# A graph network's first convolution: every 61st pair of edge blocks fetched row by row from ScalarE's queue

## What is computed

```python
def gcn_conv(x, src, dst, W, b, n):
    h = x @ W
    s, d = concatenate([src, arange(n)]), concatenate([dst, arange(n)])
    dinv = rsqrt(max(degree(d), 1))
    msg = h[s] * (dinv[s] * dinv[d])[:, None]
    return segment_sum(msg, d, n) + b
x1 = relu(batch_norm(gcn_conv(x, src, dst, W1, b1, n), g1, be1))   # 256 -> 128
x2 = relu(batch_norm(gcn_conv(x1, src, dst, W2, b2, n), g2, be2))  # 128 -> 64
out = relu(concatenate([x, x1, x2]) @ Wfc + bfc)
```

## Time and profile before

| | us |
|---|---|
| median of 3 runs | 8550.78 |
| lowest and highest | 8532.67, 8573.71 |
| the profiled execution's own time | 8529.07 |
| its span, first to last instruction | 8527.4 |
| busy in the span: PE, PE weight loads, DVE | 4861.2, 3596.1, 3516.2 |
| busy in the span: ACT, POOL | 2055.2, 4850.5 |
| mean granted TensorE clock | 0.691 of full speed |

### The profile page before, as it was taken

One profiled execution on the slowest core, in us unless ns is written; L12 is line 12 of the kernel. 1 busy time (PEld: TensorE's weight loads), 2 busy tenths in 40 slices (PEclk: granted clock), 3 DMA queues, 4 the chain that ended last, 5 costly groups with the idle time before them and its releaser, 6 DMA issues. The chain is left out here.

```text
span 8527.4 us, 116975 instructions
## 1 busy us (share of the span) xinstructions
PE 4861.2 (57%) x27409; PEld 3596.1 (42%) x27410; DVE 3516.2 (41%) x8745; ACT 2055.2 (24%) x5831; POOL 4850.5 (57%) x4806
## 2 busy tenths in 40 slices
PE   3677777777777777843343343333544444444444
PEld 2444555444555445542333333333434434444434
DVE  6565665556655556671222222222312222222224
ACT  4444554444444445550000000000100000000001
POOL 2644444444444444456666666666366666666665
PEclk9788888888888888985555555555655555555555
DMA  7654454445444545451111111111211111111114
GB/s 221 207 145 142 143 145 143 144 141 146 142 143 144 146 143 148 139 154 53 46 46 46 46 45 46 46 46 46 53 28 29 29 29 29 29 29 29 30 25 134
DMA packets 515807, 783.35 MB, mean 92 GB/s; under 512 B 143368, under 2 KB 392453, under 8 KB 514957
## 3 DMA queue, kind: packets, MB, share of 16 engines
q0 software_dynamic: 176176, 377.82, 17.4%
q1 hardware_dynamic: 303390, 369.82, 13.9%
q10 hardware_dynamic: 35758, 30.37, 1.1%
HBM read 695.07 MB, written 82.51 MB: 91 GB/s over the span
## 5 line engine op out<-in xcount | busy, mean ns | idle before, releaser
L1703 POOL DMA_INDIRECT c_g<-conv_table,c_idx x3128 | 3029.1, 968 | 1640.4 <-issue 897.0
L1782 PE MATMUL c_sums<-c_g,acc 128*128 x7040 | 1660.7, 399 | 2108.5 <-issue 1488.6
L1010 POOL DMA_INDIRECT acc<-gat_table,ga_idx x1564 | 1539.4, 984 | 1754.2 <-DVE ga_wg L1271 1252.3
L1782 PEld LDWEIGHTS c_sums<-c_g,acc 128*128 128x128 f32 x7040 | 1499.6, 299 | 2367.2 <-issue 2313.0
L1744 DVE TENSOR_TENSOR acc<-acc,c_sums 128x128 f32 (+1 forms) x1760 | 443.8, 252 | 3420.7 <-DMA ga_h<-h_parts 1111.7
L1396 PE MATMUL ga_sums<-ga_wg,ga_S 128*128 128x265 f32 x3520 | 1160.3, 454 | 266.1 <-issue 226.0
L1346 PE MATMUL ga_dstp<-ga_oht,ga_h 128*128 128x256 bf16 x5280 | 859.9, 303 | 338.5 <-DVE ga_prod L1192 199.7
L1396 PEld LDWEIGHTS ga_sums<-ga_wg,ga_S 128*128 128x128 f32 x3520 | 692.8, 218 | 504.8 <-issue 348.7
L1346 PEld LDWEIGHTS ga_dstp<-ga_oht,ga_h 128*128 128x128 bf16 x5280 | 558.1, 108 | 721.4 <-issue 279.5
L1050 ACT ACTIVATE acc<-ga_encp 128x512 f32<-128x512 f32 x880 | 518.8, 589 | 1338.6 <-remote 793.8
L1192 DVE SCALAR_TENSOR_TENSOR ga_prod<-acc,ga_a_dst,ga_dstp 128x512 f32<-128x512 f32 x880 | 647.6, 736 | 248.8 <-issue 167.8
(11 more groups left out here) (253 smaller groups left out, 3826.7 us busy)
## 6 DMA issues: line engine op xcount, KB each, us to landing
ga_h<-h_parts SPq DMA_DIRECT2D x880, 192.0 KB
ga_dl<-dl_rows SPq DMA_DIRECT2D x110, 512.0 KB
c_g<-conv_table,c_idx POOLq DMA_INDIRECT x3128
acc<-gat_table,ga_idx POOLq DMA_INDIRECT x1564
h_parts<-h_split SPq DMA_DIRECT2D x14, 1344.0 KB
gat_table<-h_out SPq DMA_DIRECT2D x14, 952.0 KB
x_rows<-md_x SPq DMA_DIRECT2D x14, 896.0 KB
fc_x<-x_rows ACTq DMA_DIRECT2D x98, 128.0 KB
```

Of the source, the lines that this page charges most:

```text
L1010: pool.indirect_dma_start(G[:, (v * PC + j) * HROW:(v * PC + j + 1) * HROW], None, gat_table, bass.IndirectOffsetOnAxis(idx[:, c:c + 1], 0 ...
L1703: pool.indirect_dma_start(G[:, c % (2 * SLOTS), :], None, table, bass.IndirectOffsetOnAxis(idx[:, c:c + 1], 0)).then_inc(rows_in[c // 2 % ...
L1782: last = nc.tensor.matmul(sums[:, b % R, 0:width], S[:, u * CH + 2 * b + j, :], flat[:, bass.ds(slots[b] * (2 * width) + j * width, width) ...
```

## The change

It concerns the first convolution alone; the second runs the code as before.

- Of the 782 pairs each one whose number is 60 modulo 61 (12 pairs: 60, 121, ... 731) is a "single"; the other 770 stay with POOL, which issues 1540 gathers, not 1564. G gets two more slots, 20 and 21, which the singles use in turn.
- ACT fetches a single in 256 DMAs of one row of 512 B, each from the row whose number is in a register. It first loads the 256 numbers into SBUF in two small DMAs (L1706 of the changed kernel), and takes them from there into registers, eight at a time (L1652). From the third single on it waits until PE has done the single two before, whose buffer it takes.
- SP's loop is written out. The same releases and announcements follow each other in straight code, with the free numbers loaded eight at a time. Right after the announcement of the pair ahead of a single, SP waits for all 256 rows of it (a semaphore that rises by 4096 each time) and announces it.
- The unit table gets a fifth row, the slot number with the singles taken out of the ring; 21 more small DVE operations in `units_phase` work it out, chained one after another. PE reads that row in c1.
- The free list of c1 leaves the singles out of the blocks and has them at its end; it comes in three DMAs, and the three rows of the table in three.

The diff, cut:

```diff
+SPAN = 61
+POOLED = [p for p in range(PAIRS) if p % SPAN != SPAN - 1]
+SINGLY = [p for p in range(PAIRS) if p % SPAN == SPAN - 1]
+PBLOCKS = -(-len(POOLED) // PB)
+PFREE = PBLOCKS + len(SINGLY)
...
-    unit_table = dram("unit_table", (4, UNITS), I32)
+    unit_table = dram("unit_table", (5, UNITS), I32)
...
-            conv_phase(nc, sb, ps, sem, pair, held, const, lists, "c1", F1, acc1, conv1_table, flat)
+            conv_phase(nc, sb, ps, sem, pair, held, const, lists, "c1", F1, acc1, conv1_table, flat, src=A["src"])
...
+                def whole(out_f, in_f, mul):
+                    link(nc.vector.tensor_scalar(out_f, in_f, float(mul), None, ALU.mult))
+                    link(nc.vector.tensor_copy(spans_i[:, :], out_f))
+                    link(nc.vector.tensor_scalar(spans_i[:, :], spans_i[:, :], RING_SHIFT, None, ALU.arith_shift_right))
+                    link(nc.vector.tensor_copy(out_f, spans_i[:, :]))
+
+                whole(spans_f[:, :], pair_f[:, :], SPAN_MUL)
+                link(nc.vector.scalar_tensor_tensor(single[:, :], spans_f[:, :], -float(SPAN), pair_f[:, :], ALU.mult, ALU.add))
+                link(nc.vector.tensor_scalar(single[:, :], single[:, :], float(SPAN - 1), None, ALU.is_equal))
...
+                nc.vector.tensor_tensor(table[:, 4, :], apart[:, :], pooled[:, :], ALU.add)
...
-        free_f = sb(ctx, f"{name}_free_f", [1, BLOCKS])
-        free_row = sb(ctx, f"{name}_free", [1, BLOCKS], I32)
-        G = sb(ctx, f"{name}_g", [P, SLOTS * 2, width])
+        apart = src is not None
+        free_f = sb(ctx, f"{name}_free_f", [1, PFREE if apart else BLOCKS])
+        free_row = sb(ctx, f"{name}_free", [1, PFREE if apart else BLOCKS], I32)
+        G = sb(ctx, f"{name}_g", [P, (SLOTS + 2 * apart) * 2, width])
+        if apart:
+            numbers = [sb(ctx, f"{name}_numbers{e}", [1, 2, P], I32) for e in range(2)]
+            numbers_in = [[sem(f"{name}_numbers{e}{u}_in") for u in range(2)] for e in range(2)]
+            single_in = [sem(f"{name}_single_in{u}") for u in range(2)]
+            s_single_ends = sem(f"{name}_single_ends_in")
...
+        def fetch_numbers(eng, e, n):
+
+            if n < len(SINGLY):
+                at = SINGLY[n] * PAIR + e * P
+                eng.dma_start(numbers[e][0:1, n % 2, :], src[at:at + P].rearrange("(o r) -> o r", o=1)).then_inc(numbers_in[e][n % 2], 16)
+
+        def fetch_row(eng, e, n, r, number):
+
+            at = SLOTS + n % 2
+            eng.dma_start(G[r:r + 1, 2 * at + e, :], table[bass.ds(number, 1), :]).then_inc(single_in[n % 2], 16)
+
+        def open_single(act, n, count):
+
+            for e in range(2):
+                act.wait_ge(numbers_in[e][n % 2], 16 * (n // 2 + 1))
+            if n >= 2:
+                free = load_frees(nc, free_row[0:1, PBLOCKS + n - 2:PBLOCKS + n - 1], mybir.EngineType.Activation)
+                act.reg_alu(count, free[0], 1, ALU.max)
+                act.wait_ge(sum_done, count)
+                take_waits(act, held)
+
         with nc.Block() as block:
             @block.sync
             def _(sp):
+                count = count_register(nc, f"{name}_sp_count", mybir.EngineType.SP)
+
+                def watch_with_singles():
+                    said, singles, frees = 0, 0, []
+
+                    def announce_next(said, singles):
+                        sp.wait_ge(rows_in[said % SLOTS], 32 * (said // SLOTS + 1))
+                        sp.sem_inc(rows_ready, 1)
+                        if singles < len(SINGLY) and POOLED[said] + 1 == SINGLY[singles]:
+                            sp.wait_ge(single_in[singles % 2], 16 * PAIR * (singles // 2 + 1))
+                            sp.sem_inc(rows_ready, 1)
+                            return said + 1, singles + 1
+                        return said + 1, singles
+
+                    for b in range(PBLOCKS + LEAD):
+                        if NB <= b < PBLOCKS:
+                            if (b - NB) % 8 == 0:
+                                frees = load_frees(nc, free_row[0:1, b:min(b + 8, PBLOCKS)], mybir.EngineType.SP)
+                            sp.reg_alu(count, frees[(b - NB) % 8], 1, ALU.max)
+                            sp.wait_ge(sum_done, count)
+                            sp.sem_inc(ring_free, 1)
+                        if b >= LEAD:
+                            for _ in range(min(PB, len(POOLED) - said)):
+                                said, singles = announce_next(said, singles)
+                    assert said == len(POOLED) and singles == len(SINGLY)
+
                 def announce(b, r):
 
                     for k in range(PB * b, PB * b + PB):
                         sp.wait_ge(rows_in[k], 32 * (r + 1))
                         sp.sem_inc(rows_ready, 1)
 
...
+                    SB = (SPAN - 1) // PB
+                    many = (PBLOCKS - NB) // SB
+                    left = PBLOCKS - NB - many * SB
+                    with nc.allow_non_contiguous_dma(reason="one small table"):
...
+                    sp.dma_start(table_row[0:1, 0:1, :], AP(unit_table.tensor, 0, [[0, 1], [UNITS, 1], [1, UNITS]])).then_inc(s_lists, 16)
+                    sp.dma_start(table_row[0:1, 1:2, :], AP(unit_table.tensor, 4 * UNITS, [[0, 1], [UNITS, 1], [1, UNITS]])).then_inc(s_lists, 16)
...
-                for b in range(NB - LEAD):
-                    announce(b, 0)
-                with sp.Fori(1, BLOCKS // NB) as i:
-                    regs = load_frees(nc, free_row[0:1, bass.ds(NB * i, NB)], mybir.EngineType.SP)
-                    for v in range(NB):
-                        release(regs[v])
...
+                if apart:
+                    watch_with_singles()
...
+                    for q, p in enumerate(POOLED):
+                        if q >= SLOTS and q % PB == 0:
+                            pool.wait_ge(ring_free, (q - SLOTS) // PB + 1)
+                        for j in range(2):
+                            pool.indirect_dma_start(G[:, q % SLOTS * 2 + j, :], None, table,
+                                                    bass.IndirectOffsetOnAxis(idx[:, 2 * p + j:2 * p + j + 1], 0)).then_inc(rows_in[q % SLOTS], 16)
+                for b in range(0 if apart else BLOCKS):
...
+                def _(act):
+                    count = count_register(nc, f"{name}_act_count", mybir.EngineType.Activation)
+                    act.wait_ge(s_free, 1)
+                    for n in range(2):
+                        for e in range(2):
+                            fetch_numbers(act, e, n)
+                    for n in range(len(SINGLY)):
+                        open_single(act, n, count)
+                        for e in range(2):
+                            for row in range(0, P, 8):
+                                regs = load_row_numbers(nc, numbers[e][0:1, n % 2, row:row + 8], mybir.EngineType.Activation)
+                                for r in range(8):
+                                    fetch_row(act, e, n, row + r, regs[r])
+                            fetch_numbers(act, e, n + 2)
 
             if fc:
...
-                dve.wait_ge(s_lists, 32)
+                dve.wait_ge(s_lists, 48 if apart else 32)
```

More of the change, by code:

```diff
@@ L198, in units_phase @@
     assert all(n * RING_MUL >> RING_SHIFT == n // SLOTS for n in range(UNITS)) and UNITS * RING_MUL < 1 << 24
+    SPAN_MUL = (1 << RING_SHIFT) // SPAN + 1
+    assert all(n * SPAN_MUL >> RING_SHIFT == n // SPAN for n in range(UNITS)) and UNITS * SPAN_MUL < 1 << 24
     GROUPED = UNITS // UL
@@ L220, in units_phase @@
         block_i = sb(ctx, "un_block_i", [P, UQ], I32)
-        table = sb(ctx, "un_table", [P, 4, UQ], I32)
+        table = sb(ctx, "un_table", [P, 5, UQ], I32)
+        spans_f = sb(ctx, "un_spans_f", [P, UQ])
+        spans_i = sb(ctx, "un_spans_i", [P, UQ], I32)
+        single = sb(ctx, "un_single", [P, UQ])
+        pooled = sb(ctx, "un_pooled", [P, UQ])
+        apart = sb(ctx, "un_apart", [P, UQ])
         base = sb(ctx, "un_base", [P, UQ])
@@ L1615, in load_frees, with load_row_numbers, conv_phase @@
     return regs
-def conv_phase(nc, sb, ps, sem, pair, held, const, lists, name, width, acc, table, work, fc=None):
+def load_row_numbers(nc, row, eng):
+    _, regs = nc.values_load_multi_w_load_instructions(
+        row, engines=[eng], min_val=0, max_val=NODES - 1,
+        skip_runtime_bounds_check_because="numbers of source nodes")
+    return regs
+def conv_phase(nc, sb, ps, sem, pair, held, const, lists, name, width, acc, table, work, fc=None, src=None):
     iota_row = const[0]
@@ L1663, in announce @@
                         sp.sem_inc(rows_ready, 1)
-                count = count_register(nc, f"{name}_sp_count", mybir.EngineType.SP)
                 def release(used):
@@ L1698, in _ @@
                 pool.wait_ge(s_idx, 16)
-                for b in range(BLOCKS):
+                if apart:
+                    for q, p in enumerate(POOLED):
[5 more added lines that the diff above has]
+                for b in range(0 if apart else BLOCKS):
```

(6 more changed lines are left out.)

51 lines of the change are left out of this document (38 added, 13 removed).

## The result

| | before | changed |
|---|---|---|
| median, us | 8546.35 (4 runs) | 9436.49 (4 runs) |
| lowest and highest | 8532.67, 8573.71 | 9427.24, 9461.31 |
| span of the profiled execution | 8527.4 | 9427.1 |
| first convolution, first to last gather begun | 2235.6 | 3139.5 |

The changed kernel is slower by 890 us: ratio 1.1067, 95% interval 1.1036 to 1.1099. The forecast was 8520, the range 8440 to 8640. The first convolution alone has the difference: its gathers span 904 us more, the rest of the program 4 us less.

A forecast was written before the change was run, and what follows sets the result against it. POOL's chain of gathers was taken to set the first convolution's length, partly through waits for PE's late sums. Saving 32 us on POOL and adding 2 gave -30 us, so 8520 us from the median 8550.78; range 8440 to 8640.

The forecast's parts named there:

- POOL, -30 to -34 us: First convolution: 24 gathers fewer on POOL save 30.0 us at undisturbed pace, 34.3 at mean pace; 32 taken.
- ACT's row at 0.46 us: First convolution: each one-row fetch on ACT costs 0.46 us, a single 137 us, hidden within 171.6 us of POOL's gathers.
- SP's 0.70 and 1.4 us: Earlier trace, SP's queue: loop loads 0.70 us in the median, single register-addressed DMAs up to 1.4; not taken as ACT's price.
- The tipping point at 0.60 us a row: First convolution: ACT's fetching costs nothing while a row stays under 0.60 us; past that ACT is the bound.
- ACT's rows are too slow: Rival, first convolution: at 0.70 us a row SP stops at the single, then POOL at the ring; 8770 us, chance 0.12.
- SP's straight code at nothing: First convolution: writing out SP's loop costs nothing, since SP waits 1635 of 2235 us for sums.
- The rival by which the loop's turns cost POOL time: Rival "more comes free", first convolution: without SP's loop and with two extra buffers POOL stalls less; 8465 us, chance 0.22.
- the stall of the earlier trace: First convolution: POOL waits 3.59 us after a gather at 4808.27 until PE's burst; read as the consumer coming late.
- The wait for a whole single, "passed before SP comes to it": First convolution, SP: at 137 to 155 us of ACT's time a single is ready before SP's wait; no cost.
- The start and the units stage, 2 us: Units stage: 21 more chained DVE operations, 4.3 us, partly covered by idling, so 2 us; SP's extra loads cost nothing.
- Why PE's sums come late while POOL gathers: First convolution: PE's late bursts fill the ring and stall POOL; their cause could not be read from the trace.

The follow-up runs named there:

- quick session: Session in which the unchanged kernel before took 6917 or 6925 us; the changed kernel run again there took 6896.21 against 6925.12, ratio 0.9957.
- held one: Session in which the unchanged kernel before took 8522 to 8621 us; the changed kernel run again in three such gave 1.1055, 1.1080 and 1.1023.
- stage (c): Short stage added behind the kernel before's end: POOL gathers 96 times, 40 semaphore instructions each on ACT, SP, DVE and PE; 1.40 us an instruction after the first dozen.
- (d): Short stage added behind the kernel before's end: POOL gathers 96 times while ACT runs its semaphore instructions in a loop; slowed by the gathers.
- stages (j) and (k): Short stages behind the kernel before's end: chains of 24 small dependent operations, POOL idle (j) or gathering (k); a PE step took 0.91 and 5.60 us.

## Why the prediction was wrong

By its steps:

- **POOL, -30 to -34 us.** Right. 1540 gathers, 29 us gained in the quick session, 47 with the rows left out in a held one, whose interval (-22 to -54) holds the 34.
- **ACT's row at 0.46 us, "ACT's rows never show that, so I take ACT's".** This step failed. In the quick session it is right (133 us a single for 137). In the session of the result a row took 1.66 us while POOL gathered, so that a single took 248.5 us, a third of them with POOL stopped, where the time for it was 171.6; undisturbed it takes 360 to 400. The rows I took the price from could not show it: the one-row DMA and the loads of the earlier trace rows stand in stages without unbroken gathers, and the 98 DMAs under POOL's gathers each come after a wait, three instructions at a time, which by stage (c) is within the first dozen that run at the usual pace. I set SP's 0.70 and 1.4 us aside as SP's own. The trace before had them on PE's queue as well (L1777 above, up to 1.403); only DVE's stood at its usual 40 ns throughout, in instructions that again stand a few at a time behind a wait. They were the price of any queue that would run long beside the gathers.
- **The tipping point at 0.60 us a row.** Right in kind: with time for 360 to 400 us (4 singles, 492 us each) the fetch is hidden in a held session too, and with 349 us (6 singles) it isn't.
- **The rival "ACT's rows are too slow".** The mechanism, the order of the waits (SP at the single, then POOL at the ring) and the sign were those of the result. Its size was not: 0.70 us a row gave 8770, where it was 1.66 until POOL stopped and 0.51 then. By the rival's own working, a single as measured, 248.5 us from one start to the next (4097.55 to 4346.08), makes 12 x 248.5 = 2982 us of the 3139.5. And it had 0.12, with a range that ended at 8640; with SP's slow rows taken as ACT's price, slow rows would have been the forecast.
- **SP's straight code at nothing.** Right in the quick session, 1.001 alone. The rival by which the loop's turns cost POOL time is out there; in a held session it is bounded by what the variant without singles gained beyond its gathers, 47 less 34 us, or 54 less 30 at the ends. In the stall of the earlier trace rows SP's slow loop end (from 4801.85 to some 4808) lies ahead of a wait for PE's sum that lasted to 4812.5, and so did not set the stall's end. The Trainium skill ("Runtime: NRT & Kernel Launch", section "Instruction fetch mechanics") says that a taken branch out of the prefetched window stalls an engine. No run here shows such a stall by itself; stages (c) and (d), straight code and a short loop, were slowed alike, by the gathers.
- **The wait for a whole single, "passed before SP comes to it".** It fell with the row price: 1041.5 us in it.
- **The start and the units stage, 2 us.** Right: DVE's list is read at 91.59 for 89.13, 2.5 us later, and the table's first load, now of one row, takes SP 0.41 us in place of 3.21.
- **Why PE's sums come late while POOL gathers**, which the prediction left open. The semaphore events of the trace narrow it down. In the stall of the earlier trace rows the unit before it is this row:

```profile
4801.93 1.22 PE L1782 MATMUL c_sums<-c_g,acc 128*128 x4 [4.42 <-issue]
```

  It ends at 4803.14, but its increment of `sum_done` comes at 4810.97; DVE's add follows at 4811.19 and PE at 4811.72. So 7.8 of the 8.58 us that PE stood are between a matmul's end, as the profile has it, and its increment. It is no single case: up to the last gather of the first convolution the recorded increments come 1.5 us (median) and up to 9.8 us after the latest such end. In both quick sessions (the variant with straight code, the changed kernel) every one comes 0.01 us after it, and in stages (j) and (k) one kernel shows both. With PE's waits thinned out the median stays, 1.7 us, which fits that this change gained 0.2%. The stalls and the slow queues belong to the same sessions and the same neighbour, the gathers; what delays the increments, and whether it is the same thing that slows the queues, is not shown.

## What to carry to other kernels

Price the instructions of an idle engine's queue from whatever queue works in the same stretch under the same neighbours, not from that engine's own rows elsewhere, and above all not from rows that each follow a wait. A fetch moved beside another one has a deadline: compute the time for it and the worst price seen on any queue, and if the two cross, the range must go there. Row-by-row fetching costs three queue instructions a row, so it suffers most when each of them slows.

## What the runs showed of the hardware

- Beside POOL's unbroken indirect gathers (one each 1.25 us) the queues of ACT, SP, DVE and PE fell to 1.40 us an instruction, after the first 12 of a stream on ACT, 14 on DVE and 17 on PE. The four together were seen in one session (stage (c)); ACT's or PE's rows show records up to 1.40 us in all five held sessions and none over 0.05 us for PE's register instruction in the quick ones. With a gather each 2.23 us, with plain DMAs from POOL or SP, or with memsets the stream was not slowed.
- In the first convolution of the kernel before (held) the increments of `sum_done` came up to 9.8 us after the latest matmul's recorded end while POOL gathered, 1.5 us in the median; in the quick sessions all came 0.01 us after it.
- The state belongs to the session: 6917 and 6925 us or 8522 to 8621 for the same program, on what is named the same chip in two of them. In the quick ones the attention layer's gathers too are done in 2219 us (317.0 to 2535.7, in the variant with straight code) where they took 3288 (315.1 to 3603.3, in the kernel before).
- The mean granted clock hardly tells them apart: 0.691 over the kernel before in the held session of the result, 0.691 to 0.694 over the same kernel in the quick ones.
- What serves the instructions and is taken up by the gathers, I can't say from these runs.
